# A recurrent attention unit's instructions put in another order on four engines of one core

## The chip, the cores and the metric

The kernel runs on one core of a Trainium2 chip. The metric is the device time of one execution in microseconds (us). The kernel before was timed in three executions; one further execution was profiled, and all durations below are of that one. Engines are named as the profile names them: PE (TensorE matmul), PEld (its weight loads), DVE (VectorE), ACT (ScalarE), POOL (GpSimd), SP (the queue that issues the DMAs).

## The reference, cut to what matters

Three layers act on x of 4 x 512 tokens with 512 features: half a feed-forward layer whose weights are a cubic spline of control points, a gated delta-rule attention layer, and half a feed-forward layer again. The change lies in the attention layer:

```python
qkvz = (x @ W_qkvz)                      # per key head: q, k (128 each), 2 x v, 2 x z (128 each)
q, k, v = silu(conv4(concat(q, k, v)))   # causal convolution of 4 taps per channel
q = inv_scale ** 2 * rms_norm(q); k = inv_scale * rms_norm(k)
beta = sigmoid(b_gate); g = -exp(A_log) * softplus(a_gate + dt_bias)
def step(S, inp):                        # one token at a time, per value head
    S = S * exp(g_t)
    delta = (v_t - k_t @ S) * beta_t
    S = S + k_t outer delta
    return S, q_t @ S
out = silu(z) * (rms_norm(out) * norm_w)
x = x + out @ W_out
```

## The kernel before, in words

`spline_phase`, `ffn_phase`, `norm_phase`, `attn_phase` and `ffn_phase` again run one after the other. `attn_phase` takes the scan by **units**: one unit is one key head with its two value heads and one sequence of the batch, 16 x 4 = 64 units. The 512 tokens of a sequence are 4 chunks of 128. Inside a chunk the recurrence is the inverse of a triangular matrix, which is built by doubling in 7 levels.

Five engines each run a program written out by hand (`pe_pass`, `act_pass`, `dve_pass`, `pool_pass`, `sp_pass`); they meet only at semaphores, and each engine takes its own instructions strictly in the written order. So the order of the code is the order of the work. The loop `for j, ... in slots()` runs over units; in turn j the engines work on the inverse and the recurrence of unit j (`has_delta`), prepare unit j+1 (`has_prep`) and finish unit j-1 (`behind`).

**The steps.** Steps s = 2 to 13 alternate between the two value heads, g = s % 2, and go up a level every two steps. In each, PE makes a *product* (4 matmuls of 128x128 f16 into the one bank `at_prod`), DVE multiplies that bank by a mask into `at_pm` (L2033, "the mask"), PE *applies* it (8 small matmuls, L1657 and L1659) and ACT copies the result (L1850), which the product two steps on reads. Behind a product, PE runs the tasks of `fill[s]`, then waits for `d_p`, the mask, and applies. What stands in `fill[s]` is therefore what hides the mask from PE. The tasks are:

- projections (`proj_part`, matmuls of 128x512 into the two banks `at_proj`): 12 per block, for k, q, v0, v1, z0, z1;
- `out_sums`: the 8 sums of squares of the unit before, one column each, into `at_proj0`; it needs the k convolution to have left that bank (`d_conv`);
- `out_product(i)`, i = 0 to 7: 3 matmuls into the one bank `at_misc`; each needs `out_add(i-1)` on DVE (L2007) to have read the bank (`d_y`);
- `turn_k`: the transposed k, into the same bank `at_misc`.

**Between the steps.** After step 13 come the residual and a Newton step, `turn_kn` (needs `a_kn`, the scaled keys of ACT, which need POOL's root of the sums that ACT's `square_k` made), and then the four chunks of the recurrence with the tasks of `gap[]`: among them `decay(0)` and `decay(1)`, which multiply the masked gates that POOL writes (`mask_g`, L2181). Behind chunk 3, PE projects 7 of the 12 q matmuls of the next unit and opens the bank of value head 1 with `level_0(j + 1, 1)`. That bank and `at_prod` held the outputs, so it waits for ACT's squares of both (`a_sqo`, L1856) and for DVE's gates (`d_gate`, L2074).

**Around the outputs on the other engines.** DVE ends its turn with the three taps of the k convolution (L1954), then gates both heads. ACT squares head 1, then head 0; it squares head 0 only when DVE has gated it. POOL splits the weights of the next key head into high and low parts once every four units: `split_wo` (j % 4 == 0, 2 x 2 instructions) and `split_part(kh+1, 2)` (j % 4 == 3) stand ahead of `mask_g(1)`.

```python
if h < R - 1:
    wait(act, "d_gate", R * j + h + 1)          # L1855: head 0 is squared after its gate
wait(pe, "d_conv", 4 * j + 1 if has_prep else 4 * j - 1)   # L1574: out_sums after the k convolution
```

## Time and profile before

| what | value |
|---|---|
| median of the 3 timed runs | 3993.65 us (3990.28 to 3993.7) |
| the profiled execution, its own time | 3988.65 us |
| its span, first to last instruction | 3986.9 us |
| what lies around the span | 1.75 us |
| PE busy | 3711.7 us, 93% of the span |
| POOL / DVE / ACT busy | 59% / 61% / 50% |
| mean granted TensorE clock | 0.963 of full speed |

A row of the timeline gives the start (us from the span's start), the duration, engine, line, operation, output and inputs with shapes, the count and, in brackets, how long the engine sat idle before it and who released it. A matmul's duration reaches over the start of the next; what a matmul costs PE is the distance from its start to the next one's start. One matmul bank written by 8 f32 matmuls of one column stands there as x16, two passes each.

### The profile page before, as it was taken

The numbers are of one execution on the slowest core, as the hardware profiler recorded it, in microseconds if no ns is written. First come the engines' busy times: TensorE is split into PE (matmuls) and PEld (weight loads), VectorE is DVE, ScalarE is ACT, GpSimd is POOL, SyncE is SP. The second block draws the span as 40 slices with busy tenths as digits, with TensorE's granted clock in tenths as the row PEclk, the third lists the DMA queues.
The fourth block names the chain that finished last, engine by engine and source line by source line (L and its number), as shares of the span: only waits on it lengthen the run. The fifth ranks groups of instructions, "written<-read, shape, count | busy, mean of one in ns | idle before, by whom it ended". The sixth has DMA issues, their size and how long they took to land. (4 is left out here: it accounts for less than half of the span.)

```text
span 3986.9 us, 74528 instructions
## 1 busy us (share of the span) xinstructions
PE 3711.7 (93%) x28324; PEld 2984.8 (75%) x28324; DVE 2447.1 (61%) x4347; ACT 1986.3 (50%) x4272; POOL 2344.9 (59%) x2805
## 2 busy tenths in 40 slices
PE   5995699999999999999999999999999999998798
PEld 4884477777777777777777777777777777776587
DVE  4654366666666666666666666666666666664464
ACT  3432355555555555555555555555555555553243
POOL 2102567676766666676676767676767676763110
PEclk8997799999999999999999999999999999998899
DMA  4333100000000000000000000000000000001521
GB/s 165 97 33 67 50 22 23 23 23 22 23 22 23 22 23 22 23 22 23 22 23 22 23 23 23 22 23 22 23 22 23 19 22 22 25 16 36 175 54 33
DMA packets 142384, 140.32 MB, mean 35 GB/s; under 512 B 84176, under 2 KB 115152, under 8 KB 140880
## 3 DMA queue, kind: packets, MB, share of 16 engines
q1 hardware_dynamic: 136992, 120.16, 10.6%
q0 software_dynamic: 4464, 14.36, 1.0%
q8 instruction: 230, 3.77, 0.4%
q14 instruction: 122, 1.00, 0.1%
q10 hardware_dynamic: 576, 1.03, 0.1%
HBM read 109.11 MB, written 26.21 MB: 34 GB/s over the span
## 5 line engine op out<-in xcount | busy, mean ns | idle before, releaser
L1850 ACT ACTIVATE at_t<-at_inv 128x512 f16<-128x512 f32 x768 | 459.0, 598 | 783.0 <-PE at_inv L1659 783.0
L1458 PE MATMUL at_proj<-x_hi,at_w_hi 128*128 128x512 f32 x1536 | 669.4, 436 | 15.7 <-POOL at_w_lo L2103 15.7
L1458 PE MATMUL at_proj<-x_lo,at_w_hi 128*128 128x512 f32 x1536 | 663.4, 432 | 0.0
L1458 PE MATMUL at_proj<-x_hi,at_w_lo 128*128 128x512 f32 x1536 | 651.9, 424 | 0.0
L2033 DVE TENSOR_TENSOR at_pm<-at_prod,at_cst 128x512 f16<-128x512 f32 x768 | 529.6, 690 | 158.3 <-PE at_prod L1458 143.7
L2007 DVE SCALAR_TENSOR_TENSOR resid<-at_misc,at_fr,resid 128x512 f32<-128x512 f32 x512 | 383.3, 749 | 137.3 <-PE at_misc L1458 134.1
L1458 PE MATMUL at_prod<-at_t,at_nlhi 128*128 128x128 f16 x3584 | 377.5, 223 | 0.9 <-DVE at_pm L2040 0.9
L1657 PEld LDWEIGHTS at_inv<-at_pm,at_t 128*128 128x128 f16 x3072 | 214.0, 101 | 218.7 <-DVE at_pm L2033 139.0
L1458 PEld LDWEIGHTS at_proj<-x_hi,at_w_hi 128*128 128x128 f32 x1536 | 299.5, 195 | 55.3 <-issue 15.9
L1458 PEld LDWEIGHTS at_proj<-x_hi,at_w_lo 128*128 128x128 f32 x1536 | 301.8, 196 | 43.1
L1458 PEld LDWEIGHTS at_proj<-x_lo,at_w_hi 128*128 128x128 f32 x1536 | 303.6, 198 | 34.0
L1657 PE MATMUL at_inv<-at_pm,at_t 128*128 128x64 f16 x3072 | 298.6, 198 | 11.4 <-DVE at_pm L2033 3.8
L2181 POOL TENSOR_TENSOR at_gt_lo<-at_cst,at_gates 128x512 fp32r<-128x512 f32 x256 | 261.9, 1045 | 77.0 <-PE at_misc L1458 77.0
L1954 DVE SCALAR_TENSOR_TENSOR at_cv_v<-at_proj,at_cw,at_cv_v 128x511 f32<-128x511 f32 (+2 forms) x384 | 287.5, 749 | 15.5 <-ACT at_cv_v L1776 2.0
L1659 PE MATMUL at_inv<-at_t,at_pm 128*128 128x64 f16 x3072 | 292.1, 196 | 0.0
L1458 PEld LDWEIGHTS at_prod<-at_t,at_nlhi 128*128 128x128 f16 x3584 | 240.6, 100 | 19.5 <-issue 18.5
L2054 DVE SCALAR_TENSOR_TENSOR at_t<-at_t,at_dcy,at_inv 128x128 f32<-128x128 f32 x256 | 77.6, 345 | 286.1 <-PE at_inv L1458 277.8
L889 PE MATMUL f_ring<-f_x_hi,ffn_w 128*128 128x512 f32 x640 | 247.2, 401 | 3.9 <-DVE f_x_lo L815 2.9
L1899 ACT ACTIVATE at_t<-at_inv 128x256 f32<-128x256 f32 x256 | 98.5, 385 | 303.5 <-PE at_inv L1716 273.5
L1910 ACT ACTIVATE at_t<-at_inv,at_gates 128x128 f32<-128x128 f32 x512 | 160.0, 364 | 175.3 <-PE at_inv L1458 175.3
L1458 PE MATMUL at_misc<-at_wo_hi,at_gt_hi 128*128 128x512 f32 x512 | 232.3, 454 | 10.5 <-DVE resid L2007 9.1
L1659 PEld LDWEIGHTS at_inv<-at_t,at_pm 128*128 128x128 f16 x3072 | 218.6, 100 | 0.0
(282 smaller groups left out, 9512.3 us busy)
## 6 DMA issues: line engine op xcount, KB each, us to landing
at_gb<-decays SPq DMA_DIRECT2D x64, 512.0 KB, 3.7
at_e<-w_qkvz SPq DMA_DIRECT2D x32, 512.0 KB, 3.7
ffn_weights<-ffn_w SPq DMA_DIRECT2D x1, 11776.0 KB, 36.8
ffn_w<-ffn_weights POOLq DMA_DIRECT2D x4, 2688.0 KB, 23.5
at_gb<-w_qkvz SPq DMA_DIRECT2D x16, 512.0 KB, 3.6
at_gb<-w_out SPq DMA_DIRECT2D x16, 512.0 KB, 3.5
f_xnext<-x_in SPq DMA_DIRECT2D x4, 1024.0 KB, 5.2
f_xres<-x_res SPq DMA_DIRECT2D x4, 1024.0 KB, 5.2
```

Of the source, the lines that this page charges most:

```text
L889: return nc.tensor.matmul(out, lhsT, rhs, start=start, stop=stop)
L1458: return nc.tensor.matmul(out, lhsT, rhs, start=start, stop=stop)
L1657: nc.tensor.matmul(half_of(ch(psT[g], c), level, 0), ch(t16[:, g, 1], c), half_of(ch(pm[:, g], c), level, 0), start=False, stop=True, skip ...
L1659: last = nc.tensor.matmul(half_of(ch(psT[g], CH + c), level, 1), ch(pm[:, g], c), half_of(ch(t16[:, g, 1], c), level, 1), start=False, sto ...
L1850: own["a_t"].up(A(grown(t16[:, s % R].rearrange("p a t -> p (a t)"), s // R), grown(psT[s % R], s // R), ACT.Copy))
L1899: own["a_v"].up(A(vp, psV, ACT.Copy))
L1910: own["a_d"].up(A(delta[:, h, :], ch(psY, h), ACT.Copy, scale=gcur[:, 2, at + c, h:h + 1]))
L1954: ins = V.scalar_tensor_tensor(out[:, s:S], unit_bank[u][:, 0:S - s], cw[(j + 1) // B % 2][:, u, 3 - s:4 - s], out[:, s:S], ALU.mult, ALU.add)
L2007: own["d_y"].up(V.scalar_tensor_tensor(row, out_bank[:], fr[:, h, c:c + 1], row, ALU.mult, ALU.add))
L2033: own["d_p"].up(V.tensor_tensor(pm[:, g].rearrange("p (c t) -> p c t", c=CH), psP[:].rearrange("p (c t) -> p c t", c=CH), mask.unsqueeze(1 ...
L2054: ins = V.scalar_tensor_tensor(state[:, h, :], state[:, h, :], dcy[:, h, c:c + 1], ch(psU, h), ALU.mult, ALU.add)
L2181: last = G.tensor_tensor(gm[:, k], incl.unsqueeze(1).to_broadcast([P, CH, P]), new_gates[:, g, at:at + CH, h:h + 1].to_broadcast([P, CH, P ...
```

## The change

- **DVE:** of the k convolution only the first tap stays ahead of the gates; taps 2 and 3 come behind both gates, as the last instructions of the turn. `out_sums` moves from step 2 to step 3, and both products of q and k (L1977) with it. The q taps move from steps 4, 5, 6 to 4, 6, 8 and stand ahead of `out_add` there. `out_add(i)` moves from step 5 + i to step 4 + i. The gate of z0 moves from step 10 to step 12.
- **PE:** `out_sums` moves from step 2, which now has no task, to step 3, ahead of the five q projections. `out_product(i)` moves from step 5 + i to 4 + i; the z projections are dealt out anew around them, 48 matmuls in steps 4 to 13 as before (step 4 now has 7 in place of 5, step 7 has 5 in place of 6, step 12 has 2, step 13 has 4). `turn_k` moves from step 13 to 12.
- **ACT:** tanh of q from step 7 to 9, tanh of z0 from 8 to 10, `square_k` from 13 to 12.
- **POOL:** `mask_g(1)` comes ahead of the weight splits; each split is cut in two halves, one behind the causal mask (`affine_select`) of each head's decays. (In the first turn, `split_part(0, 2)` stays ahead.)

Where the outputs end and a unit's steps begin, DVE's rows (`at_cv_k` is the k convolution, `at_cv_z` the gates, `at_pm` the masks, `at_aqk` the products of q and k), before:

```order
L1954 SCALAR_TENSOR_TENSOR at_cv_k<-at_proj,at_cw,at_cv_k 128x511
L1954 SCALAR_TENSOR_TENSOR at_cv_k<-at_proj,at_cw,at_cv_k 128x510
L1954 SCALAR_TENSOR_TENSOR at_cv_k<-at_proj,at_cw,at_cv_k 128x509
L2074 SCALAR_TENSOR_TENSOR at_cv_z<-at_inv,at_nw,at_cv_z 128x512
L2074 SCALAR_TENSOR_TENSOR at_cv_z<-at_prod,at_nw,at_cv_z 128x512
L2033 TENSOR_TENSOR at_pm<-at_prod,at_cst 128x512
L1995 SCALAR_TENSOR_TENSOR at_sso<-at_proj,at_qs 128x8
L1977 SCALAR_TENSOR_TENSOR at_aqk<-at_misc,at_e 128x512
L2033 TENSOR_TENSOR at_pm<-at_prod,at_cst 128x512
L1977 SCALAR_TENSOR_TENSOR at_aqk<-at_misc,at_e 128x512
```

and in the change:

```order
L1948 SCALAR_TENSOR_TENSOR at_cv_k<-at_proj,at_cw,at_cv_k 128x511
L2065 SCALAR_TENSOR_TENSOR at_cv_z<-at_inv,at_nw,at_cv_z 128x512
L2065 SCALAR_TENSOR_TENSOR at_cv_z<-at_prod,at_nw,at_cv_z 128x512
L1948 SCALAR_TENSOR_TENSOR at_cv_k<-at_proj,at_cw,at_cv_k 128x510
L1948 SCALAR_TENSOR_TENSOR at_cv_k<-at_proj,at_cw,at_cv_k 128x509
L2024 TENSOR_TENSOR at_pm<-at_prod,at_cst 128x512 x2
L1989 SCALAR_TENSOR_TENSOR at_sso<-at_proj,at_qs 128x8
L1971 SCALAR_TENSOR_TENSOR at_aqk<-at_misc,at_e 128x512 x2
```

Two taps now stand between the gates and the first mask, and nothing between the first two masks.

The same place on PE (`at_inv` the inverse, first its opening by `level_0`, then the applications; `at_proj<-at_cst,at_aqk` the output sums), in the change, with the eight rows of an application given once:

```order
L1458 MATMUL at_inv<-at_pm,at_cst 128x512
L1589 MATMUL at_inv<-at_cst,at_pm 128x128 x4
L1458 MATMUL at_prod<-at_t,at_nlhi 128x128 x4
L1651 MATMUL at_inv<-at_pm,at_t 128x32x2
...
L1653 MATMUL at_inv<-at_t,at_pm 128x32x2
L1458 MATMUL at_prod<-at_t,at_nlhi 128x128 x4
L1458 MATMUL at_proj<-at_cst,at_aqk 128x1 x8
L1458 MATMUL at_proj<-x_lo,at_w_hi 128x512
```

Before, the row of the sums stood between the first product and its application; now an application follows its product with nothing between, and the sums and five projections stand together behind the second product.

POOL in a turn with j % 4 == 0 (`at_gt_lo` the masked gates, `at_wo_hi` and `at_wo_lo` the split, `at_e` the decays), in the change:

```order
L2176 TENSOR_TENSOR at_gt_lo<-at_cst,at_gates 128x512 x2
L2196 AFFINE_SELECT at_e<-at_e 128x512
L2105 CAST at_wo_hi<-at_gb 128x512
L2106 TENSOR_TENSOR at_wo_lo<-at_gb,at_wo_hi 128x512
L2196 AFFINE_SELECT at_e<-at_e 128x512
L2105 CAST at_wo_hi<-at_gb 128x512
L2106 TENSOR_TENSOR at_wo_lo<-at_gb,at_wo_hi 128x512
```

Before, the four rows of the split stood ahead of the first of these.

The diff (hunks on PE, ACT, DVE and POOL in that order):

```diff
--- before.py
+++ after.py
@@ -1595,28 +1595,22 @@
                 fill = {s: [] for s in range(STEPS + 2)}
                 gap = {g: [] for g in range(3 * CH)}
                 if behind:
-                    fill[2].append(lambda: out_sums(j - 1))
+                    fill[3].append(lambda: out_sums(j - 1))
                 if has_prep:
                     fill[3].append(parts(Q_U, 7, 12))
-                if has_delta:
-                    fill[4].append(parts(Z0_U, 0, 5))
-                    fill[5].append(parts(Z0_U, 5, 6))
-                    fill[6].append(parts(Z0_U, 7, 8))
-                    fill[7].append(parts(Z0_U, 9, 10))
-                    for k in range(5):
-                        fill[8 + k].append(parts(Z1_U, 2 * k, 2 * k + 1))
-                if behind:
-                    for i in range(WPROD):
-                        fill[5 + i].append(lambda i=i: out_product(i, j - 1))
-                if has_delta:
-                    fill[5].append(parts(Z0_U, 6, 7))
-                    fill[6].append(parts(Z0_U, 8, 9))
-                    fill[7].append(parts(Z0_U, 10, 12))
-                    for k in range(5):
-                        fill[8 + k].append(parts(Z1_U, 2 * k + 1, 2 * k + 2))
-                    fill[13].append(parts(Z1_U, 10, 12))
+                ahead = {4: (Z0_U, 0, 3), 5: (Z0_U, 4, 5), 6: (Z0_U, 6, 7), 7: (Z0_U, 8, 9), 8: (Z0_U, 10, 11),
+                         9: (Z1_U, 0, 1), 10: (Z1_U, 2, 3), 11: (Z1_U, 4, 5), 12: (Z1_U, 6, 8)}
+                after = {4: (Z0_U, 3, 4), 5: (Z0_U, 5, 6), 6: (Z0_U, 7, 8), 7: (Z0_U, 9, 10), 8: (Z0_U, 11, 12),
+                         9: (Z1_U, 1, 2), 10: (Z1_U, 3, 4), 11: (Z1_U, 5, 6), 13: (Z1_U, 8, 12)}
+                for s in range(4, STEPS):
+                    if has_delta and s in ahead:
+                        fill[s].append(parts(*ahead[s]))
+                    if behind and s < 4 + WPROD:
+                        fill[s].append(lambda i=s - 4: out_product(i, j - 1))
+                    if has_delta and s in after:
+                        fill[s].append(parts(*after[s]))
                 if has_prep:
-                    fill[13].append(turn_k)
+                    fill[12].append(turn_k)
                     fill[14].append(parts(V0_U, 0, 4))
                     fill[15] += [parts(V0_U, 4, 9), sums]
                     gap[0].append(parts(V0_U, 9, 12))
@@ -1868,11 +1862,11 @@
                 if has_prep:
                     steps[3].append(lambda: tap(Q_U))
                     steps[4].append(lambda: tanh(K_U))
-                    steps[7].append(lambda: tanh(Q_U))
+                    steps[9].append(lambda: tanh(Q_U))
                 if has_delta:
-                    steps[8].append(lambda: tanh_z(Z0_U))
+                    steps[10].append(lambda: tanh_z(Z0_U))
                 if has_prep:
-                    steps[13].append(square_k)
+                    steps[12].append(square_k)
                     steps[14].append(square_q)
                 if has_delta:
                     steps[14].append(lambda: tanh_z(Z1_U))
@@ -2008,22 +2002,19 @@
 
                 steps = {s: [] for s in range(STEPS)}
                 if behind:
-                    steps[2].append(lambda: out_sums(j - 1))
+                    steps[3].append(lambda: out_sums(j - 1))
                 if has_delta:
-                    steps[2].append(lambda: qk(0))
-                    steps[3].append(lambda: qk(1))
+                    steps[3] += [lambda: qk(0), lambda: qk(1)]
                 if has_prep:
                     if not has_delta:
                         steps[3].append(lambda: conv(K_U, (1, 2, 3)))
-                    steps[4].append(lambda: conv(Q_U, (1,)))
+                    for i in range(3):
+                        steps[4 + 2 * i].append(lambda i=i: conv(Q_U, (i + 1,)))
                 if behind:
                     for i in range(WPROD):
-                        steps[5 + i].append(lambda i=i: out_add(i, j - 1))
-                if has_prep:
-                    for i in range(2):
-                        steps[5 + i].append(lambda i=i: conv(Q_U, (i + 2,)))
+                        steps[4 + i].append(lambda i=i: out_add(i, j - 1))
                 if has_delta:
-                    steps[10].append(lambda: silu_z(Z0_U))
+                    steps[12].append(lambda: silu_z(Z0_U))
 
                 for s in range(R, STEPS):
                     if has_delta:
@@ -2064,7 +2055,7 @@
                         if c == 2:
                             conv(V1_U, (1, 2, 3))
                         if c == 3 and j + 2 < UNITS:
-                            conv(K_U, (1, 2, 3), j + 1)
+                            conv(K_U, (1,), j + 1)
                 if has_delta:
                     for h in range(R):
                         if h == 0:
@@ -2072,6 +2063,8 @@
                         else:
                             wait(dve, "a_sqo", R * j + h)
                         own["d_gate"].up(V.scalar_tensor_tensor(cv_z[:, h, :], psO[h], nw[:, 0:1], cv_z[:, h, :], ALU.mult, ALU.mult))
+                if has_prep and j + 2 < UNITS:
+                    conv(K_U, (2, 3), j + 1)
                 if ends:
                     out_sums(j)
                     for i in range(WPROD):
@@ -2087,7 +2080,7 @@
                 link.up(ins)
                 pool.wait_ge(link.sem, link.n)
 
-            def split_part(kh, part):
+            def split_part(kh, part, hbs=range(HB)):
 
                 wait(pool, ("l_kq", "l_v", "l_z")[part], 16 * (kh + 1))
                 if part < 2:
@@ -2098,17 +2091,19 @@
                 else:
                     wait(pool, "s_z", 2 * B * kh)
                 at = slice(part * PART, (part + 1) * PART)
+                rows = slice(hbs[0], hbs[-1] + 1)
                 raw = w_raw2 if part == (1 if kh == 0 else 2) else w_raw
-                chain(G.tensor_copy(w_hi[:, :, at], raw))
-                own["p_w" if part < 2 else "p_z"].up(G.tensor_tensor(w_lo[:, :, at], raw, w_hi[:, :, at], ALU.subtract))
-
-            def split_wo(kh):
+                chain(G.tensor_copy(w_hi[:, rows, at], raw[:, rows]))
+                ins = G.tensor_tensor(w_lo[:, rows, at], raw[:, rows], w_hi[:, rows, at], ALU.subtract)
+                if hbs[-1] == HB - 1:
+                    own["p_w" if part < 2 else "p_z"].up(ins)
+
+            def split_wo(kh, h):
 
                 wait(pool, "l_wo", 16 * (kh + 1))
-                for h in range(R):
-                    wait(pool, "s_w", WPROD * (kh * B - 1) + CH * (h + 1))
-                    chain(G.tensor_copy(wo_hi[:, h], wo_raw[:, h]))
-                    own["p_wo"].up(G.tensor_tensor(wo_lo[:, h], wo_raw[:, h], wo_hi[:, h], ALU.subtract))
+                wait(pool, "s_w", WPROD * (kh * B - 1) + CH * (h + 1))
+                chain(G.tensor_copy(wo_hi[:, h], wo_raw[:, h]))
+                own["p_wo"].up(G.tensor_tensor(wo_lo[:, h], wo_raw[:, h], wo_hi[:, h], ALU.subtract))
 
             for j, has_delta, has_prep, behind, ends in slots():
                 nxt, kh = (j + 1) % 2, j // B
@@ -2193,14 +2188,16 @@
                     chain(G.tensor_tensor(rr[:, CH:2 * CH], ss[:, CH:2 * CH], half[:, CH:2 * CH], ALU.pow))
                     chain(G.tensor_tensor(scale[:, nxt, CH:2 * CH], rr[:, CH:2 * CH], cst[:, C_KSC + CH:C_LATER], ALU.mult))
                     own["p_rk"].up(G.tensor_tensor(qs2[:, nxt, :], scale[:, nxt, CH:2 * CH], scale[:, nxt, CH:2 * CH], ALU.mult))
-                    if j % B == 0:
-                        split_wo(kh)
-                    if j % B == B - 1:
-                        split_part(kh + 1, 2)
+                    if not has_delta:
+                        split_part(0, 2)
                     mask_g(1)
                     for h in range(R):
                         wait(pool, "a_ex", R * j + h + 1)
                         own["p_ex"].up(G.affine_select(e2[:, h, :], e2[:, h, :], [[0, CH], [1, P]], ALU.is_ge, 0.0, base=0, channel_multiplier=-1))
+                        if j % B == 0:
+                            split_wo(kh, h)
+                        if has_delta and j % B == B - 1:
+                            split_part(kh + 1, 2, range(h * HB // 2, (h + 1) * HB // 2))
                     for g in range(R):
                         wait(pool, "d_nl", R * (j + 1) + g + 1)
                         own["p_diag"].up(G.affine_select(nl[:, g, :], nl[:, g, :], [[0, CH], [1, P]], ALU.not_equal, -1.0, base=0, channel_multiplier=-1))
```

## Rows read from the trace of the kernel before

**Rows 1.** The page: the busy time of each engine.
```profile
PE 3711.7 (93%) x28324; PEld 2984.8 (75%) x28324; DVE 2447.1 (61%) x4347; ACT 1986.3 (50%) x4272; POOL 2344.9 (59%) x2805
```

**Rows 2.** PE's waits in the attention phase, 470 to 3640 us: total, times, longest.
```profile
PE at_inv L1458 <- ACT at_aqk L1856: 40.5, 63, 1.6
PE at_misc L1458 <- POOL at_gt_lo L2181: 34.0, 31, 1.3
```

**Rows 3.** Timeline of PE where a unit's steps begin, clock at full speed.
```profile
1567.95 0.40 PE L1458 MATMUL at_proj<-x_hi,at_w_hi 128*128 128x512 f32 x1
1568.97 0.38 PE L1458 MATMUL at_inv<-at_pm,at_cst 128*128 128x512 f16 x1 [0.63 <-ACT at_aqk L1856]
1569.41 0.39 PE L1458 MATMUL at_prod<-at_t,at_nlhi 128*128 128x128 f16 x4
1569.63 1.90 PE L1458 MATMUL at_proj<-at_cst,at_aqk 128*128 128x1 f32 x16
1571.39 0.19 PE L1657 MATMUL at_inv<-at_pm,at_t 128*128 128x64 f16 x1
...
1571.63 0.38 PE L1458 MATMUL at_prod<-at_t,at_nlhi 128*128 128x128 f16 x4
...
1573.07 0.20 PE L1657 MATMUL at_inv<-at_pm,at_t 128*128 128x64 f16 x1
```

**Rows 4.** Timeline of DVE there.
```profile
1565.19 2.32 DVE L1954 SCALAR_TENSOR_TENSOR at_cv_k<-at_proj,at_cw,at_cv_k 128x511 f32<-128x511 f32 x3 [0.95 <-ACT at_cv_k L1776]
1567.42 0.74 DVE L2074 SCALAR_TENSOR_TENSOR at_cv_z<-at_inv,at_nw,at_cv_z 128x512 f32<-128x512 f32 x1
1568.08 0.74 DVE L2074 SCALAR_TENSOR_TENSOR at_cv_z<-at_prod,at_nw,at_cv_z 128x512 f32<-128x512 f32 x1
1569.83 0.69 DVE L2033 TENSOR_TENSOR at_pm<-at_prod,at_cst 128x512 f16<-128x512 f32 x1 [1.01 <-PE at_prod L1458]
```

**Rows 5.** Timeline of ACT there.
```profile
1566.74 0.60 ACT L1856 ACTIVATE at_aqk<-at_prod 128x512 f32<-128x512 f32 x1 [0.16 <-PE at_prod L1458]
1568.26 0.60 ACT L1856 ACTIVATE at_aqk<-at_inv 128x512 f32<-128x512 f32 x1 [0.92 <-DVE at_cv_z L2074]
```

**Rows 6.** Timeline of PE, steps 4 to 13 of that unit and the residual behind them.
```profile
1573.32 0.38 PE L1458 MATMUL at_prod<-at_t,at_nlhi 128*128 128x128 f16 x4
...
1583.21 0.48 PE L1458 MATMUL at_misc<-at_wo_hi,at_gt_hi 128*128 128x512 f32 x1
...
1585.08 0.47 PE L1458 MATMUL at_misc<-at_wo_hi,at_gt_hi 128*128 128x512 f32 x1
...
1591.51 0.22 PE L1458 MATMUL at_prod<-at_t,at_nlhi 128*128 128x128 f16 x1
```

**Rows 7.** Timeline of DVE: an `out_add` in a later step.
```profile
1584.19 0.75 DVE L2007 SCALAR_TENSOR_TENSOR resid<-at_misc,at_fr,resid 128x512 f32<-128x512 f32 x1 [0.47 <-PE at_misc L1458]
```

**Rows 8.** Timeline of PE: the Newton step of head 1, then the keys' turn.
```profile
1595.68 0.38 PE L1458 MATMUL at_inv<-at_t,at_pm 128*128 128x128 f16 x4
1596.30 0.66 PE L1539 MATMUL at_misc<-at_cst,at_kn 128*128 128x128 f32 x4 [0.23 <-ACT at_kn L1819]
```

**Rows 9.** Timeline of POOL in a unit with a split of W_out.
```profile
1498.37 0.61 POOL L2110 CAST at_wo_hi<-at_gb 128x512 fp32r<-128x512 f32 x1
...
1502.22 2.04 POOL L2181 TENSOR_TENSOR at_gt_lo<-at_cst,at_gates 128x512 fp32r<-128x512 f32 x2
```

**Rows 10.** The page: the DMA of the decays, KB each, median us to landing.
```profile
at_gb<-decays SPq DMA_DIRECT2D x64, 512.0 KB, 3.7
```

**Rows 11.** Stretches 2.6 us behind each start of output sums: busy times, PEclk, DMA.
```profile
520.40:522.60 2.20, 2.20 (x21) 1.70 (x20) 1.98 (x4) 1.62 (x4) 2.12 (x3) 1.00 0.00 0
569.10:571.30 2.20, 2.20 (x14) 1.50 (x13) 1.28 (x3) 0.70 (x2) 2.12 (x3) 0.50 0.00 0
```

**Rows 12.** Timeline of PE: sums of the unit before and of the one behind.
```profile
1519.41 1.90 PE L1458 MATMUL at_proj<-at_cst,at_aqk 128*128 128x1 f32 x16
...
1618.29 1.45 PE L1458 MATMUL at_proj<-at_cst,at_aqk 128*128 128x1 f32 x12
```

## The prediction

> **What bounds the kernel now.** I read the page first, then PE's waits, then the timelines of PE, DVE and ACT where one unit hands over to the next, and last the granted clock unit by unit. The page says that PE is busy 93% of the span [rows 1], so whatever lengthens or shortens PE's own row of instructions moves the end; the other engines count only where PE waits for them. 63 of the 64 units are alike: an undisturbed one takes 1618.29 - 1569.63 = 48.66 us from output sums to output sums [rows 3, 12]. PE's waits name two places that the change touches: the opening of head 1's bank waits for ACT's squares, 40.5 us in 63 units, and the decays wait for POOL's masked gates, 34.0 us in 31 units [rows 2]. The fourth view is the clock: behind the output sums PE runs at 0.50 of full speed, its 1.2 GHz level, in 36 of the first 62 units, and at 2.4 GHz in the others [rows 11] (one unit at full speed and the first slow one stand there). A slow unit costs 1569.63 - 1519.41 = 50.22 us against 48.66, so 1.56 us each and 56 us in all [rows 3, 12].
>
> **The gates go first (gain).** Time 0 is the end of the seven q projections, 1567.95 + 0.23 = 1568.18 [rows 3]. The outputs are there when ACT starts its first square, 1566.74, but DVE runs the three taps of k from 1565.19 on and comes to the first gate at 1567.42; ACT squares head 0 0.10 us behind that gate's end, and PE opens the bank 0.11 us behind that square's end, at 1568.97 [rows 3 to 5]. With one tap ahead (until 1565.94) the gate starts with the outputs, at 1566.75, and ends at 1567.49; the square follows at 1567.59 until 1568.19; PE opens at 1568.30 in place of 1568.97. That is 0.67 us earlier per unit.
>
> **Step 2 loses its cover (loss, the largest term).** Before, the product of step 2 was followed by the output sums, 1571.39 - 1569.63 = 1.76 us, and the mask, ready at 1569.83 + 0.69 = 1570.52, was over long before them: PE didn't wait [rows 3, 4]. Now nothing stands there. The product is issued at 1568.30 + 0.44 = 1568.74 and takes PE 0.22; its mask can start 0.42 us behind its issue, as before, so at 1569.16, if DVE is free. It isn't: gate 1 starts at 1567.41, the two taps behind it at 1568.07 and 1568.85 (a tap and its own wait, 2.32 / 3), and the mask only at about 1569.52. It ends at 1570.21, PE applies at 1570.31. So PE stands idle from 1568.96 to 1570.31, 1.35 us; were DVE free it would still be 1.0. The application takes 1571.63 - 1571.39 = 0.24, so the second product stands at 1570.55; before 1571.63. Behind it the product's 0.19, the sums' 1.76 and the five projections, 1573.07 - 1571.63 - 0.19 = 1.25, put the next application at 1573.75, before at 1573.07 [rows 3]. With the gain of 0.67 already inside, PE is 0.68 us later: 63 x 0.68 = **+43 us**.
>
> **Steps 4 to 13 (loss).** They took 1591.51 - 1573.32 = 18.19 us [rows 6], with the same 48 matmuls of 512 columns, ten products and applications and `turn_k` in both orders. What stretches a step beyond PE's own work is the one bank of the output products: from one of them to the next pass 1585.08 - 1583.21 = 1.87 us when nothing else delays DVE (three matmuls, the `out_add`, two handovers), where a step of five matmuls needs about 1.70 [rows 6]. Before, four steps paid that. Now the products start in step 4 and run to 11 behind each other, and the taps of q, 0.77 us each like those of k [rows 4], stand ahead of the `out_add` in steps 4, 6 and 8, so the products of steps 5, 7 and 9 start 0.2 to 0.3 later. Walked step by step I get 2.18, 2.07, 1.86, 2.02, 1.86, 2.01, 1.86, 1.86, 1.49 and 1.42 to 1.49, in sum 18.63 to 18.70. I take +0.45 us: **+28 us**. Bounds: 0 (PE's work is the same) and +0.65 (each of the three collisions costs a whole tap less the slack of a step).
>
> **The keys' turn (gain).** `turn_kn` starts 1596.30 - 1595.68 = 0.62 us behind the Newton step, whose four matmuls need 0.20 [rows 8]: 0.42 us of wait. `square_k` a step sooner starts POOL's root, and ACT's scaling, a good 1.5 us earlier against PE. In two units of four POOL still works at a weight split and frees itself only about then, but PE comes 1.1 us later itself, so the wait goes: 63 x 0.42 = **-26 us**. Next in line is nothing; the matmuls of the recurrence follow.
>
> **The splits (gain).** POOL's four split instructions take 1502.22 - 1498.37 = 3.85 us ahead of the masked gates, for which PE waits [rows 9]. Behind the gates they fall into POOL's waits for ACT's decays and DVE's lower triangle. The second decay mask and the triangle come up to 2 us later, ahead of an opening of head 0's bank that has more slack than that. Gain 34.0 us [rows 2]: **-34 us**. SP's loads of the decays wait for the splits and start up to 5 us later, at about 1507.3 in that unit; they take 3.7 us [rows 10] and are first read where the next unit's outputs are done, some 5 us on, so they stay hidden. The later sums make POOL's root for `out_add` 1.1 us later, still ahead of the first `out_add` by my walk. The tanh of q and z0 and z0's gate move behind inputs that are ready and ahead of readers several steps on: nothing.
>
> Without the clock: 43 + 28 - 26 - 34 = **+11 us**.
>
> **The clock.** PE falls to 1.2 GHz behind the sums, and before it falls it has waited 0.79 us at the bank, done 0.64 us of short matmuls and then 1.76 us of one-column matmuls [rows 3]. The change puts 1.35 us of idleness, two short groups of 0.2 us each and the same sums behind each other: a longer stretch in which PE does next to nothing, so more units should fall. Between 36 and all 63 units fall, so the term lies between 0 and 27 x 1.56 = +42 us (a unit that stays slow for longer would cost more); below zero only if the fall hung on the wait at the bank alone, rival 2. I take 54 units: 18 x 1.56 = **+28 us**. The Trainium skill (TensorE: Matmul & The Clock Gate, Why this matters for your kernels) asks for no long idle gap between bursts of matmuls; the longest one here is shorter than the gap it warns of, before and after. By that rule alone this term is 0 and the kernel comes to rival 1's time. The trace disagrees already now: the clock falls in 36 units, though their wait at the bank is as short as the others'.
>
> **The sum.** 11 + 28 = +39 us on the profiled execution's 3988.65, so 4027.7. The three timed runs' median lies 5.0 above it, at 3993.65; on that median the change comes to 4032.7. I predict **4033 us**, 1.0% slower.
>
> **The rivals.** Differences under 0.2%, 8 us, are about what a measurement of this kernel can't tell from no change.
> 1. *The clock falls no more often.* Then 3993.65 + 11 = 4005 us. For it: the sums are the same, and a group of short matmuls now splits the idleness from them. Against: the rows above. With the terms' bounds this case lies between 3990 and 4018.
> 2. *The clock hardly falls any more, faster.* If the low clock comes from the wait at the bank running into the sums, the change takes the wait away (0.79 to about 0.1) and puts an application and a product at full speed between the idleness and the sums. With no slow unit: 3993.65 + 11 - 56 = 3949 us. The point from which it decides: fewer than 36 - 11 / 1.56 = 29 slow units make the kernel faster.
> 3. *Steps 4 to 13 cost nothing, faster.* If DVE absorbs the taps (the bound of 0) and the clock stays as it is: 3993.65 - 17 = 3977 us. For it: DVE sits idle 0.47 us ahead of an `out_add` in a quiet step [rows 7]. Against: the taps stand in a row with the very `out_add` that the next product awaits.
> 4. *The gates save nothing*, because DVE must finish the first tap and ACT copies for head 0 first: 0.67 x 63 = 42 us more, 4075 us. Against: the first tap ends 0.8 us ahead of the outputs [rows 4, 5].
>
> **How the numbers follow.** Forecast 0.57; rival 1 0.17; rival 2 0.07; rival 3 0.12; rival 4 0.07. The range must leave out no more than 2 in 10: its upper end takes all 63 units slow and steps at their bound, 3993.65 + 11 + 42 + 13 = 4060, and some for units that stay slow longer: 4072. Its lower end is just below rival 3: 3972. Rivals 2 and most of 4 stay outside. Faster: rivals 2 and 3, 0.19. Same: half of rival 1 and the foot of the forecast, 0.12. Slower: the rest, 0.69.
>
> **What would show it.** Right: PE at the opening of head 1's bank no longer names ACT's squares; a new wait of 1.2 to 1.4 us of PE or its loads for DVE's mask in step 2, 63 times; the masked gates and the keys gone from PE's waits; an undisturbed unit of about 49.4 us; 50 and more units at 0.50 behind the sums. Wrong: a step-2 gap under 0.8 us, steps 4 to 13 in 18.2 us, or fewer slow units than 36.

## The result and the profile after

The changed kernel takes **4023.28 us** (median of 4 runs, 4021.54 to 4024.07) against 3991.97 us before (4 runs, 3984.34 to 3993.7): a ratio of 1.0082, 95% interval 1.0064 to 1.0099. It is slower by 0.8%, about four times the bound of 0.2% that the prediction set for a difference; 4033 us was forecast. The profiled execution takes 4024.07 us, its span is 4022.3.

The page after says of the engines what [rows 1] said before, so it can't tell where 35 us came from:

```profile
PE 3756.3 (93%) x28324; PEld 3003.0 (75%) x28324; DVE 2447.8 (61%) x4347; ACT 1989.9 (49%) x4272; POOL 2362.4 (59%) x2835
```

PE has the same 28324 instructions and is busy 44.6 us longer. Some of its matmuls take longer than before, then, which points to the clock beside the waits. PE's waits in the attention phase (total, times, longest), against [rows 2]:

```profile
PE at_inv L1651 <- DVE at_pm L2024: 73.2, 70, 1.1
PE at_misc L1458 <- DVE resid L2001: 14.7, 80, 0.3
PE at_inv L1458 <- ACT at_aqk L1850: 1.6, 1, 1.6
```

The waits for ACT's squares (40.5) and for POOL's masked gates (34.0) are gone but for a single one of 1.6 us. In their place stands one for DVE's mask, 73.2 us, and a small one for the `out_add`. Where it lies the timeline of PE shows, at the place of [rows 3]; the projections that end at 1529.87 are time 0 of this unit:

```profile
1532.01 0.20 PE L1651 MATMUL at_inv<-at_pm,at_t 128*128 128x64 f16 x1 [1.12 <-DVE at_pm L2024]
...
1532.26 0.38 PE L1458 MATMUL at_prod<-at_t,at_nlhi 128*128 128x128 f16 x4
1532.48 1.90 PE L1458 MATMUL at_proj<-at_cst,at_aqk 128*128 128x1 f32 x16
...
1535.49 0.20 PE L1651 MATMUL at_inv<-at_pm,at_t 128*128 128x64 f16 x1
...
1535.74 0.39 PE L1458 MATMUL at_prod<-at_t,at_nlhi 128*128 128x128 f16 x4
...
1553.03 0.39 PE L1458 MATMUL at_prod<-at_t,at_nlhi 128*128 128x128 f16 x4
...
1554.48 0.22 PE L1458 MATMUL at_prod<-at_t,at_nlhi 128*128 128x128 f16 x1
```

The application of step 2 comes 2.14 us behind time 0 (2.13 forecast) and that of step 3 after 5.62 (5.57 forecast). DVE in the same place, against [rows 4]:

```profile
1528.51 0.75 DVE L2065 SCALAR_TENSOR_TENSOR at_cv_z<-at_inv,at_nw,at_cv_z 128x512 f32<-128x512 f32 x1 [0.88 <-PE at_prod L1458]
1529.18 0.74 DVE L2065 SCALAR_TENSOR_TENSOR at_cv_z<-at_prod,at_nw,at_cv_z 128x512 f32<-128x512 f32 x1
1529.84 1.52 DVE L1948 SCALAR_TENSOR_TENSOR at_cv_k<-at_proj,at_cw,at_cv_k 128x510 f32<-128x510 f32 x2
1531.27 0.68 DVE L2024 TENSOR_TENSOR at_pm<-at_prod,at_cst 128x512 f16<-128x512 f32 x1
```

The mask starts the moment DVE is done with the two taps (no bracket: DVE did not idle). PE's wait named "DVE's mask" is thus a wait for the taps ahead of the mask, which the diff put there.

The clock behind the sums, in stretches placed as in [rows 11]. The first unit stays at full speed, the second falls and is back some us later, the third (last two rows) is still low there:

```profile
520.60:522.80 2.20, 2.20 (x21) 1.69 (x20) 1.78 (x3) 0.94 (x2) 2.04 (x3) 1.00 0.00 0
570.20:572.40 2.20, 2.20 (x15) 1.49 (x14) 1.05 (x2) 0.00 (x0) 2.04 (x4) 0.50 0.04 4
574.00:576.20 2.20, 2.15 (x20) 1.47 (x19) 1.82 (x3) 1.06 (x2) 2.12 (x2) 1.00 0.13 45
771.60:773.80 2.20, 2.20 (x8) 1.97 (x9) 1.20 (x3) 0.00 (x0) 0.86 (x2) 0.50 0.00 0
775.00:777.20 2.20, 2.20 (x15) 1.91 (x13) 1.28 (x2) 1.18 (x2) 2.20 (x3) 0.50 0.73 237
```

Of the 62 inner units 20 stay at 2.4 GHz, 32 fall once, and 10 fall for twice as long, which no unit did before (26, 36 and none). Read from the medians of each kind, a unit that stays up takes 49.51 us, one that falls 1.4 more, and one that falls twice as long 2.9 more.

**The books.** The 62 units take 3139.5 us in sum, before 3104.0: +35.5, which is all of the span's +35.4. By terms, each the difference of medians of units at full speed, times 62: to the product of step 4 +0.72 us, +44.6; steps 4 to 13 +0.55 (18.18 to 18.73), +34; from there to the keys' turn -0.40, -25; POOL's splits -34. A whole unit at full speed is 49.51 - 48.68 = 0.83 longer (0.05 comes back behind the keys), so without the clock it is 51.5 - 34 = +17.5. The clock: 36 x 1.56 = 56 before, 32 x 1.4 + 10 x 2.9 = 74 after, +18.

### The profile page after: what moved, and what is told of

Its sections match the earlier page's. It is cut to its first block and busy times, and to the rows that moved or that the text cites. A ratio compares the mean times of both kernels' runs of the same rounds, so it can differ in the third digit from the quotient of the medians.

```text
span 4022.3 us, 74588 instructions
## 1 busy us (share of the span) xinstructions
PE 3756.3 (93%) x28324; PEld 3003.0 (75%) x28324; DVE 2447.8 (61%) x4347; ACT 1989.9 (49%) x4272; POOL 2362.4 (59%) x2835
## 5 line engine op out<-in xcount | busy, mean ns | idle before, releaser
L1458 PE MATMUL at_misc<-at_wo_hi,at_gt_hi 128*128 128x512 f32 x512 | 242.6, 474 | 27.0 <-DVE resid L2001 23.2
```

Source lines behind the costliest of these rows:

```text
L1458: return nc.tensor.matmul(out, lhsT, rhs, start=start, stop=stop)
```

## The experiments

Below, "quiet" is a unit whose matmuls all run at 2.4 GHz, and "low" one in which the granted clock falls to 0.50; both are counted over the same 62 units. The kernel before ran with each group: 3993.72, 3991.57, 3992.28 and 3990.76 us. Ratios are to it.

**1. The sums back in step 2** (the changed kernel, with one part undone).

```diff
-                    fill[3].append(lambda: out_sums(j - 1))
+                    fill[2].append(lambda: out_sums(j - 1))
```

DVE's own `out_sums` and the first `qk` go back to step 2 with them.

> The changed kernel with the output sums, and the products of q and k on DVE, back in step 2. My theory: the loss sits in the uncovered mask of step 2; with the sums there PE has work under the mask again, though it must first wait for taps 2 and 3 of k (about 0.8 us idle at the sums). Product of step 4 about 5.25 us behind the last q projection in place of 5.86: 62 x 0.6 = 38 us less, and slow units back from 42 to about 36: about 3970 us. Rival (the order of steps 4 to 13 is what costs): within 10 us of the changed kernel, 4015 to 4023.

Measured 3970.14 us (3966.94 to 3970.81), 0.9935 [0.9919, 0.9952]. That is the expected time. It beats the kernel before, so the move of the sums is the part that made the change slower: 53 us. The sum of units is 54 lower than in the change: quiet units 49.00 for 49.51, 32 us, and low units 35 + 1 double for 32 + 10 double, 22 us. The rest, now directly ahead of the sums, is this wait:

```profile
PE at_proj L1458 <- DVE at_cv_k L1948: 38.2, 62, 0.6
```

The sums now wait for the bank that the k taps read. Gates first do not take the old wait away as long as the taps must run in any case before something that PE needs.

**2. The q projections in step 2**, under the mask (the changed kernel, sums left in step 3).

```diff
                 if has_prep:
-                    fill[3].append(parts(Q_U, 7, 12))
+                    fill[2].append(parts(Q_U, 7, 12))
```

> The changed kernel with the five q projections moved from step 3 to step 2, where they cover the mask; the sums stay alone in step 3. My theory: the idle 1.1 to 1.3 us of step 2 are gone and nothing takes their place, 62 x 1.2 = 75 us less; and with projections between the wait and the sums hardly a unit runs at the low clock, 60 to 70 us less again: 3880 to 3900 us. Rival (the one-column sums alone bring the clock down): about 3945 us with 36 or more slow units.

Measured 3916.97 us (3915.0 to 3921.15), 0.9806 [0.9791, 0.9821]. Between theory and rival: the five projections fill the idle stretch, product 4 comes after 4.61 us in place of 5.87, and only 9 units are low. But not all of the 1.26 us stays: step 4 now takes 2.71 us in place of 2.17, since the first output product needs the bank that DVE's two `qk` still read:

```profile
1161.39 0.48 PE L1458 MATMUL at_misc<-at_wo_hi,at_gt_hi 128*128 128x512 f32 x1 [0.26 <-DVE at_aqk L1971]
```

**3. Only the splits moved** (the kernel before, with the diff's part on POOL).

```diff
-                    if j % B == 0:
-                        split_wo(kh)
-                    if j % B == B - 1:
-                        split_part(kh + 1, 2)
...
+                        if j % B == 0:
+                            split_wo(kh, h)
+                        if has_delta and j % B == B - 1:
+                            split_part(kh + 1, 2, range(h * HB // 2, (h + 1) * HB // 2))
```

> The kernel before with POOL's new order of the weight splits alone. My theory: PE's wait for the masked gates (34.0 us, 31 times) is gone, nothing else moves: 3992 - 34 = 3958 us. Rival (the splits only push the triangle and the opening of head 0's bank later): no change, 3985 to 3995, with a new wait of PE or ACT.

Measured 3943.35 us (3941.35 to 3946.54), 0.9871 [0.9857, 0.9886]. The units with a split come down to the quiet 48.66, as forecast, and POOL's masked gates leave PE's waits. The gain is larger than 34 us by the clock: 29 units are low for 36, 7 x 1.56 = 11 us. Nothing near the sums was touched; what changed, as far as the rows show, is the distance from one unit's sums to the next.

**4. Only the gates first** (the kernel before, with the diff's part on DVE).

```diff
                         if c == 3 and j + 2 < UNITS:
-                            conv(K_U, (1, 2, 3), j + 1)
+                            conv(K_U, (1,), j + 1)
...
+                if has_prep and j + 2 < UNITS:
+                    conv(K_U, (2, 3), j + 1)
```

> The kernel before with the gates ahead of taps 2 and 3 of k, and nothing else; sums stay in step 2. My theory: the opening of head 1's bank comes 0.6 us sooner, but the sums behind it need the k convolution out of their bank, which now ends 0.9 us later, so PE only waits at another place: sums start within 0.1 us of where they did, time within 8 us of before, 3985 to 4000. Rival (the gain of 0.67 us a unit stands): 3950 us.

Measured 4025.96 us (4025.34 to 4029.62), 1.0079 [1.0064, 1.0094]: outside the expectation. The wait did move as expected, from the opening to the sums:

```profile
1175.00 0.38 PE L1458 MATMUL at_inv<-at_pm,at_cst 128*128 128x512 f16 x1
...
1175.44 0.39 PE L1458 MATMUL at_prod<-at_t,at_nlhi 128*128 128x128 f16 x4
1176.44 1.80 PE L1458 MATMUL at_proj<-at_cst,at_aqk 128*128 128x1 f32 x15 [0.61 <-DVE at_cv_k L1954]
```

A quiet unit is only 48.87 - 48.68 = 0.19 us longer, 12 us in all. The clock did the rest: 44 units low and 5 of double length, 44 x 1.56 + 5 x 2.9 = 83 us against 56. Why 49 units fall and not 36 is not shown. The place of the idleness doesn't explain it: experiment 1 has the same wait of 0.6 us directly ahead of the sums, 62 times, and 36 low units.

**5. Only the steps and the keys' turn** (the kernel before with the diff's order of fills, taps, tanh, keys; gates, sums and splits as before).

```diff
-                    for i in range(WPROD):
-                        fill[5 + i].append(lambda i=i: out_product(i, j - 1))
+                    if behind and s < 4 + WPROD:
+                        fill[s].append(lambda i=s - 4: out_product(i, j - 1))
...
-                    fill[13].append(turn_k)
+                    fill[12].append(turn_k)
```

> The changed kernel with the gates, the sums and POOL's splits undone: only the output products, projections, taps of q, tanhs and the keys' turn stand in their new steps. My theory: steps 4 to 13 cost 0.55 us more a unit, the keys' turn gives back 0.4: 62 x 0.15 = +9 us, and the clock as before or somewhat different by the new period: 3990 to 4020 us, quiet unit 48.8. Rival (a step sooner is a gain by itself): below 3980.

Measured 3954.31 us (3951.2 to 3960.52), 0.9908 [0.9894, 0.9923]: the theory's range is missed, the rival's met. Steps 4 to 13 take 18.75 us for 18.18, the keys' turn is +0.17 for +0.57 less 0.4, and a unit without a split is 0.15 us longer, all as forecast (9 us). Two things outside these rows pay for it. PE waits for POOL's masked gates 18.8 us for 34.0, which fits the keys' root being done sooner on POOL, though no run separates it (PE's waits):

```profile
PE at_inv L1458 <- ACT at_aqk L1850: 40.6, 63, 1.6
PE at_misc L1458 <- DVE resid L2001: 26.3, 119, 2.0
PE at_misc L1458 <- POOL at_gt_lo L2173: 18.8, 31, 0.8
```

And only 17 units are low, 1 more for double length, though the opening, its wait and the sums are as before: 17 x 1.56 + 2.9 = 29 us for 56. The clock's share changes with a part that does not touch the place where it falls.

**6. Taps 2 and 3 of q behind the `out_add`** (the changed kernel): whether their place ahead of it stretches the steps. The first tap still stands ahead of the `out_add` of step 4.

```diff
-                    for i in range(3):
-                        steps[4 + 2 * i].append(lambda i=i: conv(Q_U, (i + 1,)))
+                    steps[4].append(lambda: conv(Q_U, (1,)))
                 if behind:
                     for i in range(WPROD):
                         steps[4 + i].append(lambda i=i: out_add(i, j - 1))
+                if has_prep:
+                    for i in range(2):
+                        steps[5 + i].append(lambda i=i: conv(Q_U, (i + 2,)))
```

> The changed kernel with taps 2 and 3 of q back in steps 5 and 6 and behind the output sums there. My theory: the three taps ahead of an output addition are what stretches steps 5, 7 and 9; two of them then stand behind one: steps 4 to 13 in about 18.4 us in place of 18.73, 62 x 0.3 = 19 us less, 4000 to 4008. Rival (the single bank of the output products alone stretches the steps): steps 4 to 13 stay at 18.6 to 18.8, 4018 to 4028.

Measured 4012.68 us (4008.71 to 4014.37), 1.0051 [1.0036, 1.0066]; 15 units quiet, 44 low, 3 double. The time lies between the two ranges, 10.6 us under the change: 0.09 us a quiet unit, some 6 us, and 3 or 4 us by the clock. Steps 4 to 13 take 18.65 us for 18.73, which is the rival's figure: to put the two taps behind the `out_add` is worth 0.08 us and not the 0.3 of the theory. It does not show that the taps cost nothing. In the change DVE's tap stands between the mask and the `out_add` that PE's next output product waits for:

```profile
1541.12 0.74 DVE L1948 SCALAR_TENSOR_TENSOR at_cv_q<-at_proj,at_cw,at_cv_q 128x510 f32<-128x510 f32 x1
1541.89 0.75 DVE L2001 SCALAR_TENSOR_TENSOR resid<-at_misc,at_fr,resid 128x512 f32<-128x512 f32 x1
```

```profile
1542.79 0.47 PE L1458 MATMUL at_misc<-at_wo_hi,at_gt_hi 128*128 128x512 f32 x1 [0.15 <-DVE resid L2001]
```

By the medians of quiet units, the steps behind the three taps, 5, 7 and 9, take 2.17, 2.08 and 1.95 us in the change, and steps 6, 8, 10 and 11 take 1.86 to 1.88, the pace of the one bank. Here the long steps are 5, 6 and 7, with 2.19, 2.14 and 1.91. The stretch moves with the taps and hardly shrinks; no run takes the taps out of these steps.

**7. Cover without the diff's steps** (the kernel before with gates first, splits behind the decays, sums in step 3 and the q projections in step 2).

```diff
-                    fill[2].append(lambda: out_sums(j - 1))
+                    fill[3].append(lambda: out_sums(j - 1))
                 if has_prep:
-                    fill[3].append(parts(Q_U, 7, 12))
+                    fill[2].append(parts(Q_U, 7, 12))
```

> The kernel before with the gates first, the new order of the splits, the five q projections under the mask of step 2 and the sums in step 3, but steps 4 to 13 as before. My theory: quiet unit 48.66 - 0.6 (opening) + 0.07 + nothing in step 2 = 48.1, so product of step 4 at 4.6, residual at 22.8; 62 x 0.55 = 34 and the splits' 34 less, and few slow units (under 15) in place of 36, 40 us more: about 3885 us, the fastest so far. Rival (with steps 4 to 13 as before the slow units stay): 3925.

Measured 3910.71 us (3905.98 to 3914.21), 0.9796 [0.9782, 0.9811], 26 us above the expectation. No unit is low. The mask of step 4 now stands behind the sums and both `qk` on DVE, so step 4 takes 2.20 us for 1.69, and PE waits for the keys:

```profile
PE at_misc L1539 <- ACT at_kn L1819: 25.2, 63, 0.7
PE at_inv L1657 <- DVE at_pm L2032: 22.5, 72, 0.8
```

**8. The sums issued twice** (the kernel of experiment 2, e2_q_under_mask in the expectation; the second set writes the same values again, so nothing that is computed changes, and no wait is added). This measures the disputed cause of the low clock by itself.

```diff
-                    for i in range(R * CH):
+                    for i in [*range(R * CH)] * 2:
```

> e2_q_under_mask with the 8 one-column sums issued twice behind each other (the second time writes the same values). 1.76 us of PE work a unit more, no wait added: 62 x 1.76 = 109 us by itself, 4026. My theory (the clock falls after a stretch in which PE moves few columns, idle or not): slow units from 9 to 40 and more, so 4070 to 4110 us. Rival (only waiting brings the clock down): 9 slow units or fewer, 4020 to 4030.

Measured 4064.17 us (4063.14 to 4065.19), 1.0181 [1.0164, 1.0198]: 6 us under the theory's range, with the count that it asked for. All 62 units are low, 61 once and 1 for double length, where 9 were. PE around the sums:

```profile
1238.16 0.38 PE L1458 MATMUL at_prod<-at_t,at_nlhi 128*128 128x128 f16 x4
1238.38 3.68 PE L1458 MATMUL at_proj<-at_cst,at_aqk 128*128 128x1 f32 x32
```

The stretch behind them (busy times, clock, DMA share):

```profile
1243.00:1245.00 2.00, 2.00 (x5) 1.29 (x5) 1.72 (x3) 0.54 (x1) 1.92 (x3) 0.50 0.15 37
```

The row of the sums (16 matmuls in two passes each, x32) carries no bracket. In none of the 62 units does PE have idle time of 0.15 us or more between time 0 and the fall: 3.68 us of one-column matmuls bring the clock down without a wait. The 147 us over experiment 2 are (3.68 - 1.90) x 63 = 112 for the second set itself, 53 x 1.1 = 58 for the clock (a low unit in experiment 2 is 49.86 us for 48.73), less some 25 of waits for DVE that the second set hides.

**9. Cover, and the keys and `qk` moved** (called e10 in the expectations that follow; the kernel of experiment 7, called e7 there, plus the diff's keys' turn, plus the second `qk` in step 4).

```diff
-                    fill[13].append(turn_k)
+                    fill[12].append(turn_k)
...
-                    steps[13].append(square_k)
+                    steps[12].append(square_k)
...
-                    steps[3] += [lambda: qk(0), lambda: qk(1)]
+                    steps[3].append(lambda: qk(0))
+                    steps[4].append(lambda: qk(1))
```

> The q projections in step 2, sums in step 3, gates first and splits behind the decays on the kernel before (3910.7 us) plus two things: the keys turned and squared a step sooner, and the second product qk of DVE in step 4 in place of 3. That kernel waited 25.2 us for the keys' scaling (63 times) and 22.5 us for DVE's mask (72 times). Theory: both waits go, and the rest is TensorE's own work: 3865 to 3880 us, no slow unit. Rival: as in the change itself, turning the keys sooner only moves their wait into the steps (the change gained 0.38 us of the 0.42 there), and the mask is late through the out_add and not the product qk: 3895 to 3910 us.

Measured 3926.19 us (3925.45 to 3927.02), 0.9839 [0.9826, 0.9853]: slower than experiment 7, outside both ranges. The wait for the keys' scaling did go, and steps 4 to 6 take 5.64 us for 6.11, but step 12 takes 3.09 us for 1.78. PE's waits, then its timeline there:

```profile
PE at_misc L1533 <- DVE resid L2007: 26.7, 38, 0.7
...
PE at_misc L1533 <- POOL at_cv_q L2140: 16.8, 24, 0.7
```

```profile
1519.37 0.40 PE L1458 MATMUL at_misc<-at_wo_hi,at_gt_lo 128*128 128x512 f32 x1
1519.60 0.40 PE L1458 MATMUL at_proj<-x_hi,at_w_hi 128*128 128x512 f32 x1
1520.70 0.63 PE L1533 MATMUL at_misc<-at_cst,at_cv_k 128*128 128x128 f32 x4 [0.70 <-POOL at_cv_q L2140]
```

`turn_k` writes the bank of the output products. In the order of before, the last product stands in step 12 too, so the turn waits for the `out_add` that reads it or for POOL, which has q's product to finish first. This is what the diff avoids by starting the output products in step 4: the two parts belong together, and neither can be costed alone.

**10. Experiment 9 with the gates behind all three taps again.**

```diff
-                            conv(K_U, (1,), j + 1)
+                            conv(K_U, (1, 2, 3), j + 1)
...
-                if has_prep and j + 2 < UNITS:
-                    conv(K_U, (2, 3), j + 1)
```

> The kernel e10 with the gates behind all three taps of k again, as before. Theory: with the q projections in step 2 nothing between the bank's opening and step 3 waits for DVE's taps, so the gates' order is worth its whole 0.6 us per unit: 62 x 0.6 = 37 us slower than e10, about 3905 to 3920 us, and the five projections ahead of the sums keep the clock up (fewer than 10 slow units). Rival A: the wait of 0.79 us at the bank brings slow units back (30 and more): 3950 us and over. Rival B: the gates' order is worth nothing by itself (in the kernel before it only moved the wait): within 8 us of e10.

Measured 3955.8 us (3954.85 to 3956.36), 0.9913 [0.9899, 0.9926]: 29.6 us slower than experiment 9, for 37 expected; the quiet unit is 49.61 us for 49.08. The time itself lies in the range of rival A, since experiment 9 came out slower than expected, but what rival A gives as the reason, 30 and more low units, did not happen. With cover in step 2 the gates' order is worth 30 us; with the sums there it lengthens the quiet unit by 0.19 us and the kernel by 32 us (experiment 4). All 62 units stay up with PE idle at the bank as long as in the kernel before (the product of step 2 comes after 1.23 us in both). So that idleness alone does not bring the clock down here, with five wide projections between it and the one-column matmuls.

**11. Experiment 9 with the keys back in step 13.**

```diff
-                    fill[12].append(turn_k)
+                    fill[13].append(turn_k)
...
-                    steps[12].append(square_k)
+                    steps[13].append(square_k)
```

> The kernel e10 with the keys back where the kernel before has them (turned and squared in step 13), so that their turn no longer waits in step 12 for the last out_add and the one bank that both use. In e10 step 12 took 3.09 us, in e7 1.78, while steps 4 to 6 of e10 took 5.64 us against 6.11 in e7. Theory: the product qk of head 1 in step 4 gives 0.47 us per unit on e7 and no slow unit comes back: 3910.7 - 29 = about 3882 us (3875 to 3892). Rival: the 0.47 is given back ahead of the keys' scaling, whose wait (25.2 us in e7) grows, or the clock falls in some units: 3900 us and over.

Measured 3902.84 us (3899.55 to 3908.01), 0.9785 [0.9771, 0.9798]. It is the fastest kernel of the study, 2.2% under the kernel before, though the rival's range is the one it falls in. Half of the units gain the whole 0.47 us (48.17 us for 48.65); the others gain nothing (49.05), because there POOL comes from a weight split and starts the keys' root late. POOL in such a unit (the split, then no idleness up to the root), then PE's keys' turn in a unit without a split and in that one:

```profile
771.46 1.04 POOL L2105 CAST at_w_hi<-at_e 128x1024 fp32r<-128x1024 f32 x1
772.58 2.39 POOL L2106 TENSOR_TENSOR at_w_lo<-at_e,at_w_hi 128x1024 fp32r<-128x1024 f32 x1
...
780.11 1.28 POOL L2140 TENSOR_TENSOR at_cv_q<-at_cv_q,at_th 128x512 f32<-128x512 f32 x1
781.47 0.23 POOL L2191 TENSOR_SCALAR at_rr<-at_ss 128x4 f32<-128x4 f32 x1
```

```profile
735.26 0.66 PE L1539 MATMUL at_misc<-at_cst,at_kn 128*128 128x128 f32 x4 [0.24 <-ACT at_kn L1819]
...
784.34 0.66 PE L1539 MATMUL at_misc<-at_cst,at_kn 128*128 128x128 f32 x4 [0.94 <-ACT at_kn L1819]
```

In five units the clock falls at this new, longer wait, which again stands just behind one-column matmuls (the four of the keys' sums, x8 in two passes each, with one short group between):

```profile
2143.42 1.05 PE L1458 MATMUL at_inv<-at_cst,at_sq 128*128 128x1 f32 x8
2144.33 0.38 PE L1458 MATMUL at_inv<-at_t,at_pm 128*128 128x128 f16 x4
...
2145.65 0.65 PE L1539 MATMUL at_misc<-at_cst,at_kn 128*128 128x128 f32 x2 [0.94 <-ACT at_kn L1819]
```

and the busy times of the 2 us behind it, with the clock at 0.50:

```profile
2146.20:2148.20 2.00, 2.00 (x8) 1.75 (x7) 0.00 (x0) 0.87 (x2) 1.59 (x4) 0.50 0.00 0
```

31 x 0.47 = 15 us less, and 5 x 1.5 = 8 us back: the 8 us between it and experiment 7.

## Why the prediction was right, and where it was not

The time and the sign were right, 4033 forecast and 4023 measured, and all five places were those named (the gates, step 2, steps 4 to 13, the keys' turn, the splits). By its steps:

- **The gates go first.** The opening's wait is gone, and PE opens the bank 0.19 us behind time 0 in place of 0.79, so 0.60 gained for 0.67 forecast. The caveat that the prediction did not make: put into the kernel before by itself, this gain does not exist. With the sums in step 2 the same 0.6 us is waited ahead of them (experiments 1 and 4), and it is worth 30 us where step 2 has cover (experiment 10). No run takes this part alone out of the change, where the two taps behind the gates hold up the mask.
- **Step 2 loses its cover.** +0.68 forecast, +0.72 measured, 43 and 44.6 us. The mask was forecast 1.34 us behind time 0 and starts at 1.40 (1531.27 - 1529.87), for the reason given, the two taps ahead of it. Experiment 1 undoes the move and gets 32 us of it back in quiet units (the wait of 0.6 for the taps' bank keeps the rest), experiment 2 keeps the move, covers the hole and gets it all.
- **Steps 4 to 13.** +0.45 forecast, +0.55 measured (18.73 us for a walk of 18.63 to 18.70). The walk holds step by step: 2.07, 2.02 and 2.01 us were forecast for the steps behind the taps, 5, 7 and 9, and 2.17, 2.08 and 1.95 measured; 1.86 for 6, 8, 10 and 11, and 1.86 to 1.88 measured. What the prediction left open is whether another place of the taps would avoid it: behind the `out_add`, taps 2 and 3 give back only 0.08 us (experiment 6). Its count for the kernel before was off by one: five steps there, 6, 7, 9, 10 and 11, took 1.87 us or more, not four. Experiment 5, with the sums in step 2, shows the same 18.75.
- **The keys' turn.** -0.42 forecast, -0.40 measured. That it is had only together with the output products a step sooner, which frees the bank for the turn in step 12, the prediction did not say (experiment 9).
- **The splits.** -34 us forecast; experiment 3 shows the 34, as all units with a split come down to 48.66, and 11 more through the clock. The decays' later loads did not show as a wait.
- **The clock.** This is the term that was mis-sized: +28 us forecast by 54 low units of 1.56 us, +18 measured by 32 of 1.4 and 10 of 2.9. More units fall, as forecast, but 42, not 54 ("50 and more" was the sign to look for), and a quarter of them for twice as long, which the prediction had named only in a bracket. That the term came this near is in part luck: parts that don't touch the sums move the number of low units by 7 and by 18 (experiments 3 and 5), and nothing in the rows before told how many would fall. For the same reason the prediction's own ground for more falls, the longer stretch in which PE does little, is not shown: 36 to 42 is a step of the size that other parts bring about.
- **The sum.** 9.4 us lie between 4032.7 and 4023.3: 10 too many for the clock, 6.5 too few for the units (+11 for +17.5), and 6 from the runs, whose medians lie 31.3 us apart where the profiled executions lie 35.4 apart, from a median of before that is 1.7 lower than the one shown.

Of the rivals, the third (steps cost nothing) falls with 18.73, the fourth with the opening at 0.19 us, the first with the clock's +18 us. The second (the clock hardly falls, 3949) falls too, and the runs show that its reason was wrong: the wait at the bank does not bring the clock down by itself (experiment 10: the same wait, with five wide projections between it and the sums, no low unit), the one-column matmuls can (experiment 8: twice as many, no wait near them, all 62 low).

The rule of the Trainium skill that the prediction weighed (TensorE: Matmul & The Clock Gate, Why this matters for your kernels) looks for long idle gaps of TensorE. By this rule the clock's term is zero; the trace disagrees, with +18 us here and all 62 units low in experiment 8, where no idle time of 0.15 us or more stands between time 0 and the fall.

What stays open is why, of units that are alike, some fall and some don't. Experiments 3, 5 and 6 change the number (36 to 29, 36 to 18, 42 to 47) by parts that change a unit's length elsewhere, and experiments 1 and 4, with the same wait of 0.6 us directly ahead of the same sums, have 36 and 49. No run held that length and changed the sums alone. So of two kernels whose counts differ by a dozen or so, no run can say that what stands at the sums made the difference; the 0 and the 62 are beyond that.

## What to carry to other kernels

Before a piece of work is moved, ask what it covers where it stands: 1.76 us of short matmuls hid a mask here, and the five projections that could have stood in the hole are worth 106 us by one line (experiment 2 against the change). Cost together the parts of a change that share a bank or an engine's queue: gates first loses 32 us alone and gains 30 us beside the projections in step 2, and the sooner keys' turn is a gain or a loss by what stands beside it. Try wide matmuls directly ahead of a group of one-column matmuls in place of a wait: the five kernels here that have them show 0 to 9 low units behind the sums (experiment 8, with the sums doubled, set aside), the others 18 to 49.

## What the runs showed of the chip

- A group of one-column matmuls lowers TensorE's clock behind it with no idle time of 0.15 us or more near it: 3.68 us of them, 62 low units of 62 (experiment 8). 1.90 us of them behind the same five wide projections, 9 of 62, with a wait of 0.26 us between them and the fall in six of the nine (experiment 2), and none with the steps of before (experiment 7).
- With idleness of 0.6 us one product ahead of such a group 36, 29 and 18 units are low (before, experiments 3 and 5), directly ahead of it 36 and 49 (experiments 1 and 4), and with five projections between none (experiment 10).
- The fall came also at a second place, where four one-column matmuls (two passes each, 1.05 us) are followed by one short group and a wait of 0.94 us, in 5 of 62 units (experiment 11); with a wait of up to 0.7 us there (experiment 7) it did not come in any unit.
- A low unit costs 1.1 to 1.56 us for the same work, one of double length 2.9.
